# Gated mixing on one Trainium2 core: the order of eight batches, and where the first convolution step runs

## The reference

```python
t = depthwise convolution of x over the tokens, three taps, padding 1, plus conv_b
u = x @ Wu.T + bu;   v = x @ Wv.T + bv
h = relu(x @ Wg1.T + bg1)                  # 64 features
gates = sigmoid(h @ Wg2.T + bg2)
global_out = cumsum(u * gates, axis=tokens) * (v * gates)
x = layernorm(x + t + global_out @ Wu.T[:256, :])
```

## Time and profile before

| | |
|---|---|
| median of three runs | 2820.26 us (2819.81 to 2822.13) |
| profiled execution, its own time | 2821.34 us |
| its span, first to last instruction | 2819.6 us |
| TensorE / VectorE / ScalarE / GpSimd busy | 2426.2 / 1950.7 / 1389.7 / 483.9 us |
| mean granted TensorE clock | 0.934 of full |
| the mixing stage, first matmul to last instruction | 1571.54 to 1657.27 us from the span's start |

### The profile page before, as it was taken

How to read it: one execution, slowest core, us unless ns; L and a number is a source line. 1 busy time by engine, 2 the same in 40 slices (tenths; PEclk the granted TensorE clock), 3 DMA queues, 4 the chain that set the end, 5 groups by cost and what they waited for, 6 DMA issues and landing times. The chain is left out here.

```text
span 2819.6 us, 42387 instructions
## 1 busy us (share of the span) xinstructions
PE 2426.2 (86%) x13892; PEld 1894.2 (67%) x13892; DVE 1950.7 (69%) x4433; ACT 1389.7 (49%) x3744; POOL 483.9 (17%) x406
## 2 busy tenths in 40 slices
PE   6997999979999999999699779966777775999998
PEld 5665566657777777777577657754554544888887
DVE  3664588865756576556645668856787775888887
ACT  5664477754544454454322123247777774333332
POOL 2442200020000000000023000026566562000000
PEclk9998999989999999999799889978888876999999
DMA  4001000001100110011200000010000003222222
GB/s 162 9 11 61 1 1 0 0 34 34 33 14 19 33 33 21 13 33 33 101 0 0 0 0 1 1 55 5 4 4 4 4 5 135 68 65 71 69 64 60
DMA packets 43902, 88.79 MB, mean 31 GB/s; under 512 B 7328, under 2 KB 20128, under 8 KB 42272
## 3 DMA queue, kind: packets, MB, share of 16 engines
q1 hardware_dynamic: 43808, 87.58, 9.3%
HBM read 78.65 MB, written 2.36 MB: 29 GB/s over the span
## 5 line engine op out<-in xcount | busy, mean ns | idle before, releaser
L2092 ACT ACTIVATE l3a_pr<-psum,l3a_nm 128x128 f32<-128x128 f32 (+1 forms) x512 | 207.4, 431 | 110.7 <-DVE l3a_nm L2200 110.7
L1099 ACT ACTIVATE l1a_pr<-psum,l1a_nb,l1a_rq 128x128 f32<-128x128 f32 (+1 forms) x256 | 127.3, 509 | 78.4 <-DVE l1a_nb L1185 73.3
L2200 DVE TENSOR_REDUCE l3a_nm<-psum 128x2 f32<-128x256 f32 (+1 forms) x256 | 124.7, 549 | 50.6 <-PE psum L1924 50.1
L2446 PE MATMUL psum<-l3f_x_hi,l3f_w_hi 128*128 128x512 f32 x384 | 151.5, 394 | 1.7 <-DVE l3f_w_lo L2532 1.7
L2496 ACT ACTIVATE l3f_sg<-psum 128x512 f32<-128x512 f32 x96 | 57.5, 599 | 192.6 <-PE psum L2448 192.6
L2447 PE MATMUL psum<-l3f_x_lo,l3f_w_hi 128*128 128x512 f32 x384 | 151.3, 394 | 0.0
L1361 POOL TENSOR_TENSOR l1f_acc<-l1f_t 128x512 f32<-128x512 f32 x4 | 6.3, 1574 | 838.9 <-DVE l1f_t L1427 838.9
L2448 PE MATMUL psum<-l3f_x_hi,l3f_w_lo 128*128 128x512 f32 x384 | 149.9, 390 | 0.0
L113 DVE TENSOR_TENSOR x_sb<-psum,x_sb 128x512 f32 (+3 forms) x44 | 36.7, 834 | 161.5 <-PE psum L1038 104.9
L2055 POOL TENSOR_TENSOR l3a_pr<-l3a_pr,l3a_ratio 128x256 f32<-128x256 f32 (+1 forms) x128 | 103.7, 833 | 171.4 <-DVE l3a_ratio L2209 171.4
L2045 POOL TENSOR_TENSOR l3a_pr<-l3a_pr,w_l3a_mask 128x1024 f32<-128x1024 f32 x32 | 78.0, 2439 | 316.5 <-ACT l3a_pr L2092 316.5
(11 more groups left out here) (447 smaller groups left out, 7352.0 us busy)
## 6 DMA issues: line engine op xcount, KB each, us to landing
l1a_kT<-l1a_o_dram SPq DMA_DIRECT2D x64, 256.0 KB, 2.7
l3f_cbuf<-l3f_c_rows SPq DMA_DIRECT2D x64, 192.0 KB, 2.8
w_l3f_all<-l3f_all_dram SPq DMA_DIRECT2D x1, 9216.0 KB, 24.9
l3f_cbuf<-l3f_c_rows SPq DMA_DIRECT2D x64, 128.0 KB, 2.9
w_l0f_w<-l0f_w_dram SPq DMA_DIRECT2D x2, 2048.0 KB, 10.3
l3f_cbuf<-l3f_c_rows SPq DMA_DIRECT2D x64, 64.0 KB, 2.5
w_l1f_all<-l1f_all_dram SPq DMA_DIRECT2D x1, 2560.0 KB, 9.3
cf_sb<-xT SPq DMA_DIRECT2D x9, 256.0 KB, 2.5
```

The source lines that it names most:

```text
L1099: last = nc.scalar.activation(pr[:, n % 2, i, s], S[n % 2][:, i, s], ACT.Exp, bias=nb[:, n % 2, t, i:i + 1], scale=rq[:, t, 2 * n + i:2 * ...
L2092: last = nc.scalar.activation(pr[:, r, a, g, k], S[:, g, k], ACT.Exp, bias=nm[:, i % 2, g, t:t + 1], accum_out=sums[:, r, a, g, t:t + 1])
L2200: last = nc.vector.tensor_reduce(nm[:, i % 2, 2 * pair:2 * pair + 2, t], S[:, 2 * pair:2 * pair + 2, t * P:t * P + (t + 1) * P], AX.X, ALU ...
L2446: mm(bk[n % 2], hi, x_hi[:, k, chunk], start=(k == 0), stop=False)
```

## The change

The two-batch turns and the hardware loops are gone; all eight batches are written out.

- TensorE: `front(n)` (h, u, v, gate) and `back(n)` (output) are functions. The order is front 0, then for every n: front n+1, back n. From n = 2 on a front first waits for `z_ready` at n-1.
- ScalarE: a new function `centre(n)` does the first convolution step of a batch (middle tap and bias) as an activation with the identity function; it posts `tc_ready`. From n = 2 on it waits for back n-2 (`y_ps` at n-1), which reads the buffer that it writes. It stands ahead of everything for batch 0, and after the sigmoids of batch n for batch n+1. The sigmoids wait for `mix_ready` at n-1.
- VectorE: for every n the two remaining convolution steps (after `tc_ready`), the mixing, and then the output of batch n-1. The output of batch 7 comes last.

The instructions within these pieces and their shapes are as before, but for the step that moved. No DMA is in the stage, before or after. The core of the diff:

```diff
+                def front(n):
+                    i, tokens = n % 2, slice(n * T, (n + 1) * T)
+                    if n >= 2:
+                        pe.wait_ge(z_ready, n - 1)
+                    for k in range(KD):
+                        last = mm(HY[i][0:DH, 0:T], w["g1"][:, k, :], xT[:, k, tokens], start=(k == 0), stop=(k == KD - 1))
+                    last.then_inc(h_ps, 1)
...
+                def back(n):
+                    i = n % 2
+                    pe.wait_ge(mix_ready, n + 1)
...
-                pe.sem_inc(z_ready, 2)
-                with pe.Fori(0, B // 2) as b:
...
+                front(0)
+                for n in range(B):
+                    if n + 1 < B:
+                        front(n + 1)
+                    back(n)
 
             @block.scalar
             def _(act):
+                def centre(n):
+                    if n >= 2:
+                        act.wait_ge(y_ps, n - 1)
+                    for k in range(KD):
+                        last = nc.scalar.activation(tc[:, n % 2, k, :], xT[:, k, n * T:(n + 1) * T], ACT.Identity,
+                                                    bias=w["convb"][:, k:k + 1], scale=w["conv"][:, k, 1:2])
+                    last.then_inc(tc_ready, 1)
...
+                centre(0)
+                for n in range(B):
+                    i = n % 2
+                    act.wait_ge(h_ps, n + 1)
+                    nc.scalar.activation(hT[:, i, :], HY[i][0:DH, 0:T], ACT.Relu, bias=w["bg1"][0:DH, :]).then_inc(h_ready, 1)
+                    act.wait_ge(g_ps, n + 1)
+                    if n >= 2:
+                        act.wait_ge(mix_ready, n - 1)
...
+                    if n + 1 < B:
+                        centre(n + 1)
...
-                with dve.Fori(0, B // 2) as b:
...
-                        for k in range(KD):
-                            last = nc.vector.tensor_scalar(tc[:, i, k, :], x(k, 0, T), w["conv"][:, k, 1:2], w["convb"][:, k:k + 1], ALU.mult, ALU.add)
-                        st.do(last)
...
+                def output(n):
+                    dve.wait_ge(y_ps, n + 1)
+                    add_and_measure(nc, st, x_sb, mv, n * TT, TT, two(HY[n % 2]), lw, z_ready, n + 1)
...
+                for n in range(B):
+                    convolve(n)
+                    mix(n)
+                    if n >= 1:
+                        output(n - 1)
+                output(B - 1)
```

More of the change, by code:

```diff
@@ L1463, in l2_mixing @@
         h_ready = sem("h_ready")
+        tc_ready = sem("tc_ready")
         uv_ps = sem("uv_ps")
@@ L1475, in _ @@
                 mm = nc.tensor.matmul
+                def front(n):
[5 more added lines that the diff above has]
+                    last.then_inc(h_ps, 1)
+                    for name, bk in (("u", U), ("v", V)):
+                        for m in range(2):
+                            for k in range(KD):
+                                last = mm(bk[i][:, m * T:(m + 1) * T], w[name][:, k, m * P:(m + 1) * P], xT[:, k, tokens],
+                                          start=(k == 0), stop=(k == KD - 1))
+                    last.then_inc(uv_ps, 1)
+                    pe.wait_ge(h_ready, n + 1)
+                    for m in range(2):
+                        last = mm(GG[i][:, m * T:(m + 1) * T], w["g2"][0:DH, m * P:(m + 1) * P], hT[:, i, :], start=True, stop=True)
+                    last.then_inc(g_ps, 1)
@@ new lines, in back @@
+                def back(n):
+                    i = n % 2
+                    pe.wait_ge(mix_ready, n + 1)
+                    for t in range(TT):
+                        y = HY[i][:, t * D:(t + 1) * D]
+                        for k in range(2):
+                            mm(y, go[:, i, k, t * P:(t + 1) * P], w["u"][:, k, :], start=(k == 0), stop=False)
+                        for k in range(KD):
+                            last = mm(y[:, k * P:(k + 1) * P], tc[:, i, k, t * P:(t + 1) * P], c["id"], start=False, stop=(k == KD - 1))
+                    last.then_inc(y_ps, 1)
@@ L1476, in _ @@
                 w["early"](pe)
                 w["late"](pe)
-                pe.sem_inc(z_ready, 2)
-                with pe.Fori(0, B // 2) as b:
-                    for i in range(2):
-                        x = lambda k: xT[:, k, bass.ds(b * 2 * T + i * T, T)]
-                        pe.wait_ge(z_ready, 2 * b + i + 1)
-                        for k in range(KD):
[L1484 to L1504, removed]
@@ L1508, in _ @@
                 nc.scalar.preload_act_table(ACT.Sigmoid)
+                w["early"](act)
                 w["late"](act)
[L1510 to L1517, removed]
+                centre(0)
@@ new lines, in _ @@
+                for n in range(B):
[5 more added lines that the diff above has]
+                        act.wait_ge(mix_ready, n - 1)
+                    for m in range(2):
+                        last = nc.scalar.activation(ga[:, i, m, :], GG[i][:, m * T:(m + 1) * T], ACT.Sigmoid, bias=w["bg2"][:, m:m + 1])
+                    last.then_inc(ga_ready, 1)
+                    if n + 1 < B:
+                        centre(n + 1)
@@ L1519, in _, with convolve @@
             @block.vector
             def _(dve):
-                st = Steps(dve, steps, L2A_STEPS)
+                st = Steps(dve, steps, 0)
+                st.begin(0)
+                def convolve(n):
+                    i = n % 2
+                    dve.wait_ge(tc_ready, n + 1)
+                    for k in range(KD):
+                        last = nc.vector.scalar_tensor_tensor(tc[:, i, k, 1:T], xT[:, k, n * T:(n + 1) * T - 1], w["conv"][:, k, 0:1],
+                                                              tc[:, i, k, 1:T], ALU.mult, ALU.add)
+                    st.do(last)
+                    for k in range(KD):
+                        last = nc.vector.scalar_tensor_tensor(tc[:, i, k, 0:T - 1], xT[:, k, n * T + 1:(n + 1) * T], w["conv"][:, k, 2:3],
+                                                              tc[:, i, k, 0:T - 1], ALU.mult, ALU.add)
+                    st.do(last)
@@ new lines, in mix @@
+                def mix(n):
+                    i = n % 2
+                    dve.wait_ge(uv_ps, n + 1)
+                    dve.wait_ge(ga_ready, n + 1)
+                    for m in range(2):
+                        nc.vector.scalar_tensor_tensor(ug[:, i, m, :], U[i][:, m * T:(m + 1) * T], w["bu"][:, m:m + 1], ga[:, i, m, :], ALU.add, ALU.mult)
+                        last = nc.vector.scalar_tensor_tensor(vg[:, i, m, :], V[i][:, m * T:(m + 1) * T], w["bv"][:, m:m + 1], ga[:, i, m, :], ALU.add, ALU.mult)
+                    st.do(last)
+                    for m in range(2):
+                        last = nc.vector.tensor_tensor_scan(cum[:, i, m, :], ones[:, :], ug[:, i, m, :], 0.0, ALU.mult, ALU.add)
+                    st.do(last)
+                    nc.vector.tensor_tensor(go[:, i, :, :], cum[:, i, :, :], vg[:, i, :, :], ALU.mult).then_inc(mix_ready, 1)
@@ L1556 @@
-L2A_STEPS = 2 * (5 + LN_STEPS)
+                for n in range(B):
[4 more added lines that the diff above has]
+                output(B - 1)
 def l2_ffn(nc, c, x_sb, mv, xT, w, psum):
```

## The result

The changed kernel takes 2830.14 us (median of 6 runs, 2825.96 to 2832.56) where the kernel before takes 2820.71 (6 runs, 2819.06 to 2824.69). The ratio is 1.0029, with a 95% interval of 1.0017 to 1.0042: slower by three parts in a thousand. (The two medians alone would give 1.0033; the means of the same runs, 2829.5 and 2821.2, give 1.0029.) The forecast was 2830.3.

What follows compares the result with a forecast made beforehand. Waits bound the stage, in a closed loop of mixing, addition, front and gate. 2821.34 us plus 2.47 (loop), 7.1 (clock) and 0.5 (last gap) gave 2831.4, less 1.08 for the median 2830.3; range 2822.5 to 2834.5.

Steps and rivals of the forecast that it cites:

- The loop: Mixing stage: mixing, addition of output, next front, gate, mixing form a closed chain of 11.14 us a batch, against 9.84 before.
- Head and tail: Stage ends: front 2 starts at 16.85 us, back 7 at 83.08; the stage takes 88.20 us, 2.47 more than before.
- The clock: TensorE gaps ahead of fronts 2 to 7: low clock follows three in four, 1.58 us each, 7.1 us in all.
- The half microsecond for the gap ahead of the last back: TensorE's 1.99 us gap ahead of back 7: low clock may follow, bounds 0 and 1.68 us, 0.5 taken.
- The first one: Mixing stage: loop as forecast but clock mostly stays up, at most two low stretches, 2823 to 2826 us; chance 0.15.
- The second: TensorE: straight code closes the issue gaps, up to 5.6 us gained, not slower, 2821.2 us; chance 0.07.
- The third: Mixing stage: stream bound by TensorE at 8.54 us a batch, stage 72.6 us, time 2807.2 us; chance 0.04.
- The fourth: ScalarE: identity not in the sigmoid's table set, reloads add at least 10.3 us, 2840.6 us; chance 0.03.
- The covers: Convolution step moved to ScalarE: 0.9 to 1.3 us a batch hidden in waits, no cost; VectorE's saving worth nothing.

Runs made afterwards that it cites:

- h_in_gate_bank: Changed kernel with h written into the gate's PSUM bank and the wait for the addition moved from front to back: 2809.7 us, ratio to before 0.996.
- output_before_mix: Changed kernel with VectorE doing the output of batch n-1 ahead of the mixing of batch n: 2820.71 us, ratio to before 0.9997.
- uv_first: Changed kernel with the products of u and v moved ahead of the wait and of the product of h: 2814.54 us, ratio to before 0.9974.
- fill_gap: Changed kernel with four extra matmuls of 128x256 ahead of each front from batch 2 on: 2824.41 us, ratio to before 1.0007.
- step_on_vector: Changed kernel with the first convolution step back on VectorE, new order kept: 2831.09 us, ratio to before 1.0034.
- pairs_straight: Kernel before, its order of two fronts and two backs kept, convolution on VectorE, hardware loops written out: 2821.71 us, ratio to before 1.0002.
- h_in_gate_step_on_vector: Changed kernel with h in the gate's bank and the first convolution step back on VectorE: 2807.94 us, ratio to before 0.9956.

## Why the prediction was right, point by point

**The loop.** Worked out at 11.14 us; the windows show 11.14 and 11.15 in the two turns at full clock that were not the last. Each link is in the timeline of after at its value: 6.80 from front to mixing, 3.00 to the last product, 0.61 to the addition. `h_in_gate_bank` shows that this loop and no other was the limit, and `output_before_mix` and `uv_first` that it matters what stands between the addition and the wait, each at nearly the period that the same links gave.

**Head and tail.** Front 2 came 16.83 us after front 0 (16.85 worked out), back 7 10.54 after front 7 (10.53), after an idle gap of 1.94 us (1.99) that was not followed by the low level here. From back 7 to the end it was 4.89 us instead of 3.04 + 2.08 = 5.12. So where 88.20 was worked out at full clock, these pieces give 16.83 + 5 x 11.14 + 10.54 + 4.89 = 87.96, and `fill_gap` measured 87.97.

**The clock.** 1.58 us was put for a low stretch; the windows give 1.64 to 1.66 (12.78 and 12.80 less 11.14). The frequency was put at three in four. The profile after shows three in six, `step_on_vector` four in six (the windows of 12.79, 12.83 and 12.83 us, and the last one, cut at back 7, with a mean of 0.86), before and `pairs_straight` three in four each: 13 in 20. In the profiled execution the term therefore cost 4.95 us (92.91 less 87.96) and not 7.1. Six gaps at 13 in 20 are 6.4 us, so the term was mis-sized by 0.7 us on the mean, and by 2 in the one execution that was profiled, within the range given. The half microsecond for the gap ahead of the last back was not paid in this execution; over all profiles here a gap of 1.94 us was followed by the low level five times in twelve, so 0.5 was about right. How many low stretches the other five runs of the changed kernel had is not known.

**The rivals.** The first one, at most two low stretches, is not what the profile shows, but with three in six the profiled execution (2826.3) ends just above its range of 2823 to 2826; from that one time it could not be told from the forecast. The second, issue gaps closed by straight code, is out: they stand at 3.1 and 2.7 us as before, and `pairs_straight` is at 1.0002. The third, a stream bound by TensorE, was worked out at 72.6 us for the stage and 2807: this is the kernel `h_in_gate_bank`, at 72.31 us. The order of the change is the same there; only the bank of h and the place of the wait differ. The fourth, a change of table for identity, is out: one table load, 1.28 us. The Trainium skill's rule ("ScalarE: Activation LUTs", Table sets: the hidden batching unit) that identity is in every set agrees with this.

**The covers.** The moved step took 592 ns each, inside the 0.47 to 0.62 of the bounds; it waits 1.98 us for the back and ends 1.4 us before the next front (at 1609.28, worked out at 9.8 us after the front, and it was 9.7). VectorE waits 3.87 us in a full-clock turn and not the 2.8 worked out: between the addition and the next mixing (1598.82 to 1606.35) that leaves 3.66 us of its own work, where output and convolution had been put at 4.7. The output was over-priced: the prediction puts it at 2.8, for which it shows no row, while its own tail uses 2.08 for the same work, and in this turn it took 1.96 (1598.82 to 1600.78). Nothing hung on it, since either fits the hole.

**The whole.** The profiled executions differ by 2824.5 - 2819.6 = 4.9 us, the stage by 7.18. The other 2.3 us are in code that the change doesn't touch, and go the other way. The median rose by 9.4 us and the mean by 8.3, where the forecast has 10.1 from terms that sum to 7.2 in the profiled stage. The path and both mechanisms were right; the agreement of 2830.14 with 2830.3 to 0.2 us is luck: the spread of the runs is 6.6 us.

## What to carry to other kernels

When work is reordered to overlap, walk once around the closed chain: which wait lets the new work start, what stands ahead of its release in that engine's program order, and whether this needs the new work. A buffer shared by two products can close the chain although every engine has slack. Here giving one product another bank, or swapping two blocks on one engine, was worth far more than moving an operation to an idle engine, which gave no gain clear of the noise in the time of the whole kernel. On TensorE count an idle gap twice, for itself and for the lower clock that may follow it.

## What the runs showed of the hardware

How often the low level followed an idle gap of TensorE inside the mixing stage, in the twelve profiles:

| idle gap | profiles | low level followed |
|---|---|---|
| 0.56 to 0.85 us | `uv_first`, `fill_gap`, `output_before_mix` | 0 of 20 |
| 1.94 to 1.95 us | nine, mostly ahead of the last back | 5 of 12 |
| 2.43 to 2.55 us, one of 3.04 | before, after, `step_on_vector`, `pairs_straight` | 13 of 20 |
| 5.74 us | `output_before_mix`, ahead of the last back | 1 of 1 |

Even the same code in the same loop goes either way (after: three of six). Where the work behind the gap was on the path, one low stretch cost 1.3 to 1.7 us. Filling the gaps of 2.54 us down to 0.81, with 5.4 us of matmul work in the stage, brought the ratio from 1.0029 to 1.0007, and against `step_on_vector` on the same chip it lowered the median by 6.7 us (2831.09 to 2824.41).

The code ahead of the stage is the same in all these kernels, yet the stage's first matmul started between 1568.03 and 1577.75 us. Windows of the stretch ahead of it, of `fill_gap` and of the first `h_in_gate_step_on_vector`:

```profile
0.00:1577.75 1577.75, 1414.68 (x7664) 1084.03 (x7665) 981.65 (x2408) 804.88 (x2053) 180.51 (x174) 0.96 0.08 29
```

```profile
0.00:1568.03 1568.03, 1405.71 (x7665) 1077.79 (x7665) 982.12 (x2408) 804.52 (x2053) 180.49 (x174) 0.97 0.08 29
```

TensorE is busy for 9 us longer in the one, with the same instructions (one record apart) and a mean granted clock of 0.96 instead of 0.97; VectorE and ScalarE are within 0.6 us. Why the clock differs there is open. So differences of a few microseconds between two profiles of this kernel say nothing unless they are read inside the stage that was changed.
